# Attention values multiplied in two halves, skip sums at other rows, a norm beside its rows, a last MLP in two sets of banks

## The reference, cut to what matters

```python
# x: (8, 384, 32, 32); layer 0
xn = rmsnorm over channels (x) * norm_w
global = (mamba(xn) + flip(mamba(flip(xn)))) * scale_mod     # 16 states, 1024 steps, both directions
local = sigmoid(depthwise 3x3 (xn) + dw_b) * xn
x = x + res_scale * (global + local)
# layer 1 on tokens t: (8, 1024, 384), 6 heads of 64
t = t + attention(ln(t))          # causal softmax
t = t + gelu(ln(t) @ kron(fc1, fc2).T) @ kron(pr1, pr2).T   # 1536 hidden
```

## Time and profile before

| | us |
|---|---|
| three runs: lowest, median, highest | 4295.2, 4300.12, 4302.93 |
| the profiled execution | 4300.21 |
| its span | 4298.4 |
| busy: TensorE, VectorE, ScalarE, GpSimd | 3369.9, 3586.2, 2549.2, 2733.2 |
| mean granted clock of TensorE | 0.874 |
| from the end of the last product of the last row (3960.2) to the end | 338 |

### The profile page before, as it was taken

One profiled execution on the slowest core, in us unless ns is written; L12 is line 12 of the kernel. 1 busy time (PEld: TensorE's weight loads), 2 busy tenths in 40 slices (PEclk: granted clock), 3 DMA queues, 4 the chain that ended last, 5 costly groups with the idle time before them and its releaser, 6 DMA issues.

```text
span 4298.4 us, 40497 instructions
## 1 busy us (share of the span) xinstructions
PE 3369.9 (78%) x11626; PEld 1702.9 (40%) x11626; DVE 3586.2 (83%) x2721; ACT 2549.2 (59%) x3547; POOL 2733.2 (64%) x1692
## 2 busy tenths in 40 slices
PE   5500598878888798888988798887988788876997
PEld 2200245623365234632356233642346233551472
DVE  4999698899889998899889998899888998898121
ACT  4533456756675656757566666757667566665362
POOL 2888476676766766577766767567675767666000
PEclk9755799988999798988999789997999889997998
DMA  3999598787978878787978879787987879788000
GB/s 86 233 244 248 127 223 188 189 202 197 222 165 202 218 183 209 174 204 187 238 170 201 197 194 227 175 196 187 217 196 179 205 191 234 165 201 207 6 7 15
DMA packets 224024, 785.11 MB, mean 183 GB/s; under 512 B 25292, under 2 KB 40958, under 8 KB 223518
## 3 DMA queue, kind: packets, MB, share of 16 engines
q0 software_dynamic: 117504, 427.87, 51.4%
q1 hardware_dynamic: 106270, 354.32, 25.0%
HBM read 339.60 MB, written 39.85 MB: 88 GB/s over the span
## 4 chain that ended last, share of the span: by engine, by line
PE 39%; DVE 23%; issue 12%; DMA 12%; ACT 7%; POOL 6%; DVEq 0%; ACTq 0%; SPq 0%; POOLq 0%
DVE pBC L1181 15%; PE pW L653 10%; DMA y<-hb 9%; PE pW L572 9%; POOL hb L1360 5%; PE pW L460 5%; PE pW L503 4%; ACT pt L980 3%; PE pW L588 2%; PE pW L537 2%; PE pW L710 2%; DMA y<-area 1%; DVE hb L1190 1%; PE pW L716 1%; DVE pBC L1146 1%
## 5 line engine op out<-in xcount | busy, mean ns | idle before, releaser
L1181 DVE TENSOR_TENSOR_SCAN pBC<-pBC,hb 128x1024 f32<-128x1024 f32 x768 | 1757.1, 2288 | 55.2 <-POOL hb L1360 33.7
L1371 POOL DMA_DIRECT2D y<-hb x768 | 729.3, 950 | 820.8 <-DVE hb L1190 732.7
L1360 POOL TENSOR_TENSOR hb<-du_f,b_row 128x1024 f32<-128x1024 f32 x384 | 1014.9, 2645 | 118.4 <-DMA b_row<-bc_rows 72.7
L1360 POOL TENSOR_TENSOR hb<-uc_b,b_row 128x1024 f32<-128x1024 f32 x384 | 994.8, 2591 | 66.7 <-DMA y<-hb 64.6
L1190 DVE TENSOR_TENSOR hb<-pBC,c_row 128x1024 f32<-128x1024 f32 x768 | 940.0, 1224 | 44.4
L799 ACT ACTIVATE pBC<-delta,vec 128x1024 f32<-128x1024 f32 x384 | 429.5, 1119 | 412.6 <-DVE hb L1190 412.5
L799 ACT ACTIVATE pBC<-xres,vec 128x1024 f32<-128x1024 f32 x384 | 429.3, 1120 | 323.5 <-DVE hb L1190 322.8
L653 PE MATMUL pW<-area,pt 128*128 128x64 f32 x3456 | 437.8, 281 | 138.3 <-ACT pt L980 138.3
L653 PEld LDWEIGHTS pW<-area,pt 128*128 128x128 f32 x3456 | 409.1, 194 | 192.4 <-ACT pt L980 184.1
L1225 DVE TENSOR_REDUCE stat<-pW 128x1 f32<-128x640 f32 (+7 forms) x361 | 258.5, 752 | 228.1 <-PE pW L575 228.1
L479 PE MATMUL pW<-area,xn_area 128*128 128x512 f32 x576 | 267.7, 620 | 30.9 <-DVE area L1268 22.6
(11 more groups left out here) (167 smaller groups left out, 4906.9 us busy)
## 6 DMA issues: line engine op xcount, KB each, us to landing
y<-hb POOLq DMA_DIRECT2D x768, 512.0 KB, 7.2
b_row<-bc_rows SPq DMA_DIRECT2D x256, 512.0 KB, 5.9
c_row<-bc_rows SPq DMA_DIRECT2D x256, 512.0 KB, 5.4
du_f<-in_x SPq DMA_DIRECT2D x8, 1536.0 KB, 13.0
kept_residual<-in_x SPq DMA_DIRECT2D x8, 1536.0 KB, 14.3
y<-area POOLq DMA_DIRECT2D x24, 512.0 KB, 7.9
xres<-kept_residual SPq DMA_DIRECT2D x8, 1536.0 KB, 11.9
out_x<-xa SPq DMA_DIRECT2D x8, 1536.0 KB, 7.8
```

What stands on the lines that cost most here:

```text
L1181: dve.tensor_tensor_scan(flow(d, buf), flow(d, buf), flow(d, hb[r % NHB][:, :]), 0.0, ALU.mult, ALU.add).then_inc(scan_done, 1)
L1360: pool.tensor_tensor(hb[r % NHB][:, :], du[d][:, k, :], b_row[g % 2][:, :], ALU.mult)\
L1371: pool.dma_start(y[:, k, :], hb[r % NHB][:, :], accum_op=ALU.add).then_inc(y_in[k], 16)
```

## The change

Five things are changed.

- Values (`item("values")` on TensorE): the first four blocks are multiplied as soon as the half that was transposed first has been copied, the others when the second has. Groups take turns: an even group transposes half 0 first and into bank 2, an odd one half 1 first and into bank 3 (`halves`), and values go into the bank that was transposed first (`value_bank`). Transposes of the second half wait for the scaling of the group before. In the last pass the order of halves and the bank stay, and values go by halves too.
- Skip sums (`SKIP`): at rows 24, 27 and 30. The softplus items of the backward direction for k = 1 and 2 start at rows 26 and 29, a row later than before. The key projections wait for the skip sum of their own block instead of all.
- Sample 0's `NEXT` items stand beside its rows as in the other samples (`beside`), and what ran behind its last row is taken out.
- In the head, the three local products come ahead of the gated ones.
- The last pass's MLP takes turns between `pW` and the other four banks for the hidden groups (`hidden_bank`); a hidden group waits for the gelu two groups before, and the first of the second half is issued ahead of the last product of the first half.

```diff
-RS = 21
+SKIP = (24, 27, 30)
-BEHIND = ([("step_silu", 0, 17), ("step_x", 0, 19)] + [("step_skip", k, RS - KT + k) for k in range(KT)]
-          + [(kind, k, 22 + 3 * k + i) for k in range(KT)
+BEHIND = ([("step_silu", 0, 17), ("step_x", 0, 19)] + [("step_skip", k, 18 + k) for k in range(KT)]
+          + [(kind, k, (22, 26, 29)[k] + i) for k in range(KT)
...
-    return [(kind, n) for kind, n in SLOTS[r] if kind in STEP or layer1 and (more or kind not in NEXT)]
+    return [(kind, n) for kind, n in SLOTS[r] if kind in STEP or (more if kind in NEXT else layer1)]
...
-        pBC = [ctx.enter_context(nc.psum_tensor(f"pBC{i}", [128, L], F32)) for i in range(2)]
+        pB = ctx.enter_context(nc.psum_tensor("pB", [128, 4, HALF], F32))
+        pBC = [pB[:, 2 * i:2 * i + 2, :].rearrange("p b t -> p (b t)") for i in range(2)]
...
+        def halves(b, g):
+            return (0, 1) if alone(b) or g % 2 == 0 else (1, 0)
+        def value_bank(b, g):
+            return pW[:, 3 if alone(b) else 2 + g % 2, :]
+        def hidden_bank(b, g):
+            return pB if alone(b) and (g + g // NFG) % 2 else pW
...
-            return 16 * (r // KT + 1 + (r >= RS))
+            return 16 * (r // KT + 1 + (r > SKIP[r % KT] - LAG))
...
-                for half in range(2):
+                for n, half in enumerate(halves(b, g)):
                     if g:
-                        pe.wait_ge(pt_ready, at(2 * NG, a, 2 * g - 1 + half))
-                    if g and half and not alone(b):
+                        pe.wait_ge(pt_ready, at(2 * NG, a, 2 * g))
+                    if g and n and not alone(b):
                         pe.wait_ge(ctx_ready, at(NG, a, g))
...
-                        pe.wait_ge(pt_ready, at(2 * NG, a, 2 * g + 2))
                         if alone(b):
                             pe.wait_ge(ctx_ready, at(NG, a, g))
-                        for t, (h, i, c0) in enumerate(GROUPS[g]):
-                            for j in range(i + 1):
-                                mm = pe.matmul(pW[:, 3, DH * t:DH * t + DH], pt[:, c0 + 128 * j:c0 + 128 * j + 128],
-                                               vtok[:, j, DH * h:DH * h + DH], start=(j == 0), stop=(j == i))
+                        for m, half in enumerate(halves(b, g)):
+                            pe.wait_ge(pt_ready, at(2 * NG, a, 2 * g + 1 + m))
+                            part = [(t, h, j, c0 + 128 * j) for t, (h, i, c0) in enumerate(GROUPS[g])
+                                    for j in range(i + 1) if (c0 + 128 * j) // HALF == half]
+                            for q, (t, h, j, col) in enumerate(part):
+                                mm = pe.matmul(value_bank(b, g)[:, DH * t:DH * t + DH], pt[:, col:col + 128],
+                                               vtok[:, j, DH * h:DH * h + DH], start=(m == 0 and q == 0),
+                                               stop=(m == 1 and q == len(part) - 1))
...
+                        if alone(b):
+                            pe.wait_ge(p_ready, at(NG, a, NG))
+                            pe.wait_ge(pt_ready, at(2 * NG, a, 2 * NG))
+                            if g >= 2:
+                                pe.wait_ge(h_ready, at(2 * NFG, a, g if g == NFG else g - 1))
+                        elif g:
                             pe.wait_ge(h_ready, at(2 * NFG, a, g))
-                        if q == 0 and c:
+                        if q == (1 if alone(b) else 0) and c:
                             pe.wait_ge(x2_ready, at(2, a, c))
...
-                    if q < NFG:
-                        hidden()
+                    if not alone(b):
+                        if q < NFG:
+                            hidden(g)
+                    elif g < 2 * NFG and (q or c == 0):
+                        hidden(g)
...
-                    if n == 14 and not alone(b):
-                        for k in range(KT):
-                            act.wait_ge(y_in[k], at(YIN, b, 16 * (RS // KT + 1)))
+                    if n >= 14 and n % 2 == 0 and not alone(b):
+                        k = n // 2 - 7
+                        act.wait_ge(y_in[k], at(YIN, b, 16 * ((SKIP[k] - LAG - k) // KT + 2)))
...
-                    if more and not layer1:
-                        item("next_square", 0, b, True)
-                        item("next_rstd", 0, b, False)
-                        for t in range(6):
-                            copy_u(b + 1, t)
...
+                    for k in range(KT):
+                        local(b, k)
                     if layer1:
                         gated(b - 1)
-                    for k in range(KT):
-                        local(b, k)
...
-                pool.wait_ge(y_in[k], at(YIN, b, landed(RS - KT + k)))
+                pool.wait_ge(y_in[k], at(YIN, b, 16 * ((SKIP[k] - LAG - k) // KT + 1)))
...
-                        if RS <= r < RS + KT:
-                            sum_skip(b, r - RS)
+                        if r in SKIP:
+                            sum_skip(b, SKIP.index(r))
```

More of the change, by code:

```diff
@@ L683, in item, with hidden @@
                     g = c * NFG + q
-                    toks = slice(c * HALF, (c + 1) * HALF)
-                    def hidden():
+                    def hidden(g):
+                        c, q, bank = g // NFG, g % NFG, hidden_bank(b, g)
+                        toks = slice(c * HALF, (c + 1) * HALF)
                         pe.wait_ge(xr_step, at(5, a, 5))
@@ L695, in hidden @@
                             ft = FGRP * q + f
-                            pe.matmul(pW[:, f, :], fc_bf[:, 128 * ft:128 * ft + 128], xr_a[:, toks],
+                            pe.matmul(bank[:, f, :], fc_bf[:, 128 * ft:128 * ft + 128], xr_a[:, toks],
                                       start=True, stop=False)
-                            mm = pe.matmul(pW[:, f, :], fc_bf[0:2 * KI, 128 * ft:128 * ft + 128],
+                            mm = pe.matmul(bank[:, f, :], fc_bf[0:2 * KI, 128 * ft:128 * ft + 128],
                                            xr_b[0:2 * KI, toks], start=False, stop=True)
                         mm.then_inc(fc_ready, 1)
-                    if q < NFG:
-                        hidden()
+                    if not alone(b):
[3 more added lines that the diff above has]
+                        hidden(g)
                     if q >= 1:
@@ L744, in iteration @@
                             item(kind, i, b)
-                    if more and not layer1:
-                        item("next_mean", 0, b)
-                        in_project(b + 1, 0, 6)
                     if not more:
@@ L891, in scale_ctx @@
                 for t, (h, i, c0) in enumerate(GROUPS[g]):
-                    cx = act.activation(ctxk[:, i, DH * h:DH * h + DH], pW[:, 3, DH * t:DH * t + DH], ACT.Identity,
+                    cx = act.activation(ctxk[:, i, DH * h:DH * h + DH], value_bank(b, g)[:, DH * t:DH * t + DH], ACT.Identity,
                                         scale=stat[:, 2, st + t:st + t + 1])
@@ L975, in item @@
                         g = n - 1
-                        for half in range(2):
-                            act.wait_ge(tr_ready, at(2 * NG, a, 2 * g + half + 1))
+                        for m, half in enumerate(halves(b, g)):
+                            act.wait_ge(tr_ready, at(2 * NG, a, 2 * g + m + 1))
                             if g:
@@ L1013, in item @@
                             act.wait_ge(r_done, at(2 * NFG, a, g - 1))
-                        act.activation(hid[:, g % 2, :, :], pW[:, 0:FGRP, :], ACT.Gelu).then_inc(h_ready, 1)
+                        act.activation(hid[:, g % 2, :, :], hidden_bank(b, g)[:, 0:FGRP, :], ACT.Gelu).then_inc(h_ready, 1)
                         if not alone(b):
@@ L1293, in iteration @@
                             item(kind, i, b, False)
-                    if more and not layer1:
-                        item("next_norm", 0, b, False)
                     if not more:
```

1 line of the change is left out of this document (removed).

## The result

The changed kernel takes 4224.52 us (median of four runs, 4218.09 to 4225.68) beside 4300.73 for the kernel before (4295.20 to 4302.93): a ratio of 0.982, 95% interval 0.981 to 0.984. That is 76 us less, where 115 were forecast; 4224.5 lies inside the range of 4150 to 4240 and 39.5 us above the forecast. The profiled execution took 4223.4 us, with a span of 4221.6.

What follows compares the result with a forecast made beforehand. TensorE was taken to bound rows with attention, VectorE rows without. Savings of 75 + 1 + 8 + 26 + 2 + 3 = 115 us from the median of 4300.12 gave 4185 us, range 4150 to 4240.

Steps and rivals of the forecast that it cites:

- Values by halves: Attention rows, seven samples: starting values at the first copy cuts the pitch from 5.53 to 5.12 us; -75 us.
- Loop (b): Attention rows: two-row loop through VectorE's reciprocal, ScalarE's scaling, second half's transposes, copy, exponential and scores; 5.13 us a row.
- loop (a): Attention rows: the loop scores, row maximum, exponential, next scores takes 5.07 us a row.
- Rival 1: Attention rows: VectorE becomes the bound at 4.88 us a row; -118 instead of -75, 4142 us; chance 0.10.
- rival 3: Attention rows keep their pitch, as the next group's exponential or the scaling already sets it; 4260 us; chance 0.06.
- Skip sums: Softplus rows: spreading skip sums to rows 24, 27, 30 shortens VectorE's waits for input product and logarithms; -8 us.
- Rival 2: Skip sum at row 27 costs more than it frees, 5 us more in eight samples; 4233 us; chance 0.17.
- First sample's norm: Sample 0: next norm and projections move beside rows 66 to 76; head -31, VectorE's rows +5, together -26 us.
- Local before gated: Head of a sample: VectorE's local products ahead of gated ones cut ScalarE's softplus wait; -2 us over seven samples.
- Last MLP: Last sample's MLP: a second set of banks removes TensorE's 1.63 us gelu wait, twice; -3 us.
- The last sample's values: Last pass: only the last two groups, with no scores left beside them, gain from values by halves; -1 us.
- rival 4: TensorE's clock drops to 1.2 GHz inside attention as values change banks; slower, 4377 us at 40 groups; chance 0.02.

Runs made afterwards that it cites:

- experiment 1: The kernel before with only the values by halves (order of halves, bank of the values, one wait per half): 4247.07 us, ratio 0.987.
- experiments 2: The changed kernel with skip sums back at rows 21, 22, 23 and softplus steps back at rows 22, 25, 28: 4209.85 us, ratio 0.978.
- experiment 5: The changed kernel repeated unaltered, timed beside the kernel before: 4219.45 us, ratio 0.981.
- experiment 8: The changed kernel with only ScalarE's softplus absolute values ahead of the row's projection copies, TensorE's order kept: 4218.64 us, ratio 0.981.
- experiment 7: The changed kernel with all softplus steps of a row ahead of its other items on every engine: 4249.36 us, ratio 0.988.

## Why the prediction was right, and where it was off

The direction and the range held, and the forecast's likeliest course was the one taken: values by halves carry it. But the term for the skip sums has the wrong sign. Three terms, values, skip sums and norm, make up 35 of the 39 us that are missing.

**Values by halves: -75 forecast, -66 measured** (rows 33 to 62; -58 by the times of experiment 1). The step was right down to its loops. Loop (b), through the reciprocal, was put at 5.13 us and 5.12 taken; the rows run at 5.15, and without that loop at 5.09 where loop (a) was put at 5.07. Of the 9 us that are missing, some 6 are in the pitch: a row gains 0.376 us (5.527 to 5.151) instead of 0.41. The rest is in sample 7, whose 24 rows take 1.0 us more than the others', and in the edges of the attention (rows 33, 34 and 59 to 61), which gain 4.0 us in all samples together where two more rows at the full gain, 5.7, were counted. Rival 1 (VectorE at 4.88) did not come, nor did rival 3.

**Skip sums: -8 forecast, 10 to 15 us slower measured** (experiments 2 and 5). This is the step that failed: "Queued behind are the input product of the next row, for which VectorE waits" was true, but the wait was counted as time. It lay beside the wait for the first logarithm, which ends some 14.8 us after scan 21 whether GpSimd holds the scans or not. Taking away the wait that ends first gave VectorE the other one. The forecast gain behind the logarithms went the wrong way too: with the step starting at row 26 its absolute value moved behind the copy of the first key projection, and there it waits for a chain on TensorE whose length depends on the granted clock (0.54 or 5.53 us, experiment 5). Rival 2 had the sign, at +40 instead of +10 to +15, and the wrong mechanism: its wait at row 28 exists, but in samples 1 to 7 it shows only when the logarithm is made earlier (experiment 8). In the change, it is 1.5 us in sample 0 and nothing in the others; the wait at row 32 that was put at 1 us is 3.9 us in sample 0 and at most 0.9 in the others. That the total fell inside the range owes nothing to this term.

**First sample's norm: -26 forecast, -18 to -23 measured.** The head of sample 1 is 50.6 us long (last product's end at 475.81 to scan at 526.43) instead of the loop's 47.5 that was assumed. The 47.5 was the shortest of six such heads of the trace before, which have 47.5 to 51.8 and a mean of 48.6; in the change they have 44.7 to 50.5. So sample 1's did become one of the loop's, at their upper end, and one head was too few to read the figure from. The rows grew by 7.1 instead of 5, and of that the trace shows a cause. VectorE's three products of the norm and GpSimd beside them:

```profile
373.51 3.70 DVE L1285 SCALAR_TENSOR_TENSOR area<-du_f,vec,prob 128x1024 f32<-128x1024 f32 x1
...
377.13 4.55 DVE L1285 SCALAR_TENSOR_TENSOR area<-du_f,vec,prob 128x1024 f32<-128x1024 f32 x2
```

```profile
373.47 2.64 POOL L1375 TENSOR_TENSOR hb<-uc_b,b_row 128x1024 f32<-128x1024 f32 x1
...
378.14 2.46 POOL L1375 TENSOR_TENSOR hb<-uc_b,b_row 128x1024 f32<-128x1024 f32 x1 [1.18 <-DMA y<-hb]
```

The first product starts 0.04 us after GpSimd's and ends 1.09 us after it, where one takes 1.28 us alone; the three take 8.17 us instead of the 3.68 of the earlier trace rows, where GpSimd was idle. The Trainium skill (SBUF — State Buffer, section on who interferes with whom) has VectorE operations with two SBUF inputs and GpSimd's reading operations take one shared port pair as an exclusive lock, so that the later one is blocked for the whole instruction. This trace agrees: the product ends as if it had waited out GpSimd's 2.64 us and then run. Costing a moved operation by its duration in a place where the other engine is idle was the mistake. The 4.5 us of it are more than the 2.1 by which the rows missed; what gave the rest back was not looked for.

**Local before gated: -2 forecast**; 0 to -7, not told apart from nothing. **Last MLP: -3 forecast, -6 measured** (341.6 to 335.7), at the end of its bounds of 0 to -6. The wait of 1.63 us, twice, is half of it; where the rest comes from was not tried. The last sample's values (-1 forecast) can't be told: with them and the old MLP the stretch is 340.8 and 341.6 us, without them 341.7.

Together: -66 + 12 - 20 - 6 = -80, against 76 and 84 us (4303.61 - 4219.45) in the two timings of the change.

**The clock (rival 4)** stayed at 2.4 GHz in attention. The Trainium skill (TensorE: Matmul & The Clock Gate, second failure mode) tells of a bf16 kernel whose clock goes up and down as it cycles through PSUM banks. Here, in f32 and with the values changing banks every group, rows 34 to 60 read 1.00 in all seven samples, so no trace here bears it out. The clock did matter elsewhere, in rows 21 to 33.

## What to carry to other kernels

A wait is worth only what is not beside another wait: before spreading a blocking step, ask when the next thing that its engine waits for would be ready without it, and from which engine. When an item of a fixed order is moved, look at what it comes to stand behind on every queue, for the item that it now follows may hang on a slower chain, and don't let work that waits go ahead of work that is ready (experiment 7). Edits of this kind must be tried together: the same reordering gave nothing that could be told from scatter on one base and 9 to 12 us on another.

## What was not expected of the hardware

Two executions of one program can differ by 13 us in one stretch and by 0.8 us in all. In rows 21 to 33 TensorE idles up to 2.5 us between projections, and the granted clock falls to half level in every sample with attention of both traces of the change. What varies is when and for how long. A few us behind scan 21 it stands at 0.50 for 3 to 4 us in most samples, but for 10 in two samples of the first trace and in one of the repeat. And it falls again some 24 us behind scan 21, for 10 us, in four samples of the repeat, where it stays up for longer in all others. Either long form makes the sample's rows 21 to 33 1 to 3 us longer. What decides between the forms is open: ahead of the second place TensorE idles 2.15 us both where the clock then falls and where it stays up. A profile of one execution is therefore good to some 10 us in these rows. That the old rows beat the spread ones there rests on four traces of the one (475.7 to 480.6 us, mean 478.3) and six of the other (481.7 to 495.1, mean 487.8): 9.5 us, close to the 10 to 15 of the times.

In the change the skip sum at row 27, issued behind a row sum in the same step, holds GpSimd for 4.2 to 5.9 us until that sum has landed, and the one at row 24, whose row sum was issued a row earlier, for 4.6 to 5.5. The Trainium skill (DMA: Bandwidth & Descriptors, section on the anatomy of one SWDGE DMA) would give 3.2 us for 512 KB from issue to landing, by my estimate, where the median of the profiles before and after is 7.2 as in the earlier trace rows. By that figure a row sum issued one row of 3.5 us earlier would have landed, and the skip sum at row 24 would show no wait; the traces don't agree.
